# Routed rows scattered as sorted pieces of three rows, one indirect scatter a column

## What is computed

```python
logits = jnp.einsum('bsd,de->bse', x, gate_w) + gate_b
probs = jax.nn.softmax(logits, axis=-1)
top_probs, top_idx = jax.lax.top_k(probs, 2)          # 2 of 16 experts for each token
top_probs = top_probs / jnp.sum(top_probs, axis=-1, keepdims=True)
dispatch = jnp.sum(jax.nn.one_hot(top_idx, n_experts) * top_probs[..., None], axis=-2)
h1 = jnp.einsum('bsd,edh->bseh', x, w1)               # 64 -> 128
h2 = jnp.einsum('bsd,edh->bseh', x, w2)
hidden = jax.nn.silu(h1) * h2
expert_out = jnp.einsum('bseh,eho->bseo', hidden, w3) # 128 -> 64
out = jnp.einsum('bseo,bse->bso', expert_out, dispatch)
```

## Time and profile before

| | |
|---|---|
| median of 3 runs | 790.79 us (790.71 to 795.49) |
| profiled execution, span from first to last instruction | 791.9 us; no other time of this execution is given |
| mean granted TensorE clock, share of full speed | 0.873 |
| busy TensorE / its weight loads | 578.2 / 476.0 us |
| busy VectorE / ScalarE / GpSimd | 441.7 / 347.6 / 518.2 us |

### The profile page before, as it was taken

The page is one execution under the profiler, slowest core; times in us unless marked ns, Lnnn a source line. Parts: engine busy times, 40 slices in busy tenths (PEclk is TensorE's granted clock), DMA queues, the critical chain, the costliest instruction groups (busy, mean ns, idle before and its releaser), DMA issues.

```text
span 791.9 us, 14201 instructions
## 1 busy us (share of the span) xinstructions
PE 578.2 (73%) x3856; PEld 476.0 (60%) x3856; DVE 441.7 (56%) x1237; ACT 347.6 (44%) x753; POOL 518.2 (65%) x540
## 2 busy tenths in 40 slices
PE   5967796787799989998899889998958702883000
PEld 3455545574588678867786678687958702873000
DVE  5664755556447686676667567756765601454111
ACT  2124122152456476647564566446626701674111
POOL 2052246576771777777777777777777777777774
PEclk9976796798999999999999999979979965996555
DMA  2499022333553375528542744374345414544111
GB/s 78 101 229 396 28 71 83 97 97 90 148 170 89 72 188 142 144 53 208 136 124 69 190 130 121 76 175 109 112 117 128 114 51 127 135 100 98 40 40 31
DMA packets 168871, 93.20 MB, mean 118 GB/s; under 512 B 99680, under 2 KB 152928, under 8 KB 168800
## 3 DMA queue, kind: packets, MB, share of 16 engines
q1 hardware_dynamic: 151632, 66.71, 32.1%
q0 software_dynamic: 16384, 25.20, 11.6%
q10 hardware_dynamic: 784, 0.39, 0.2%
HBM read 45.06 MB, written 47.19 MB: 116 GB/s over the span
## 4 chain that ended last, share of the span: by engine, by line
POOL 33%; PE 29%; issue 15%; DVE 13%; DMA 7%; ACT 3%; POOLq 0%; ACTq 0%; DVEq 0%; SPq 0%
POOL rows_scratch L497 15%; POOL sums L514 14%; PE wide_ps L1030 5%; PE h_ps L1169 4%; PE y_ps L1186 3%; DMA hx<-xi_scratch 3%; DMA xi_scratch<-xi 2%; POOL hx L514 2%; POOL kexp L514 2%; PE turn_ps L1153 2%; PE wide_ps L1050 2%; PE wide_ps L1129 1%; PE hidT_ps L1179 1%; PE wide_ps L1036 1%; DVE twice_y L970 1%
## 5 line engine op out<-in xcount | busy, mean ns | idle before, releaser
L497 POOL DMA_INDIRECT rows_scratch<-z_parts,place x256 | 254.9, 996 | 128.4 <-issue 74.7
L514 POOL DMA_INDIRECT sums<-y_scratch,place x224 | 213.8, 955 | 82.7 <-issue 66.4
L1169 PE MATMUL h_ps<-w_hi,rowsT 128*128 x384 | 111.5, 320 | 40.9 <-DVE hid_all L972 33.8
L970 DVE SCALAR_TENSOR_TENSOR twice_y<-tanh,h_ps 128x256 f32<-128x256 f32 x192 | 79.8, 416 | 101.3 <-ACT tanh L618 85.3
L1169 PEld LDWEIGHTS h_ps<-w_hi,rowsT 128*128 128x128 f32 x384 | 74.6, 194 | 55.8 <-issue 54.5
L1186 PE MATMUL y_ps<-w_sb,hidT_all 128*128 x768 | 100.9, 276 | 1.1 <-ACT twice_y L631 1.1
L1169 PE MATMUL h_ps<-w_lo,rowsT 128*128 x384 | 101.0, 290 | 0.0
L1186 PEld LDWEIGHTS y_ps<-w_sb,hidT_all 128*128 128x128 f32 x768 | 97.4, 199 | 2.2 <-issue 2.2
L1153 PE MATMUL turn_ps<-ident,rows_all 128*128 128x128 f32 x384 | 60.8, 282 | 46.3 <-DMA rows_all<-rows_scratch 39.8
L618 ACT ACTIVATE tanh<-h_ps 128x256 f32<-128x256 f32 x192 | 69.8, 387 | 56.3 <-PE h_ps L1169 50.0
L972 DVE SCALAR_TENSOR_TENSOR hid_all<-twice_y,h_ps 128x256 f32<-128x256 f32 x192 | 80.8, 421 | 6.6
(11 more groups left out here) (252 smaller groups left out, 910.3 us busy)
## 6 DMA issues: line engine op xcount, KB each, us to landing
rows_all<-rows_scratch SPq DMA_DIRECT2D x96, 256.0 KB
y_scratch<-twice_y SPq DMA_DIRECT2D x96, 128.0 KB
rows_scratch<-tanh SPq DMA_DIRECT2D x3, 3072.0 KB, 19.4
xi_scratch<-xi SPq DMA_DIRECT2D x16, 256.0 KB
rows_scratch<-z_parts,place POOLq DMA_INDIRECT x256
hx<-xi_scratch SPq DMA_DIRECT2D x14, 256.0 KB
sums<-y_scratch,place POOLq DMA_INDIRECT x224
out<-sums SPq DMA_DIRECT2D x56, 64.0 KB
```

The costliest lines, as they stand in the source:

```text
L497: gp.indirect_dma_start(rows_dram[n], bass.IndirectOffsetOnAxis(ap=place[m % RING][:, r, j:j + 1], axis=0), z_parts[m % 2][:, j // 2, j % ...
L514: gp.indirect_dma_start(y_of[r][apart(m)][:, j // 2, j % 2, :], None, y_dram[m % 3], bass.IndirectOffsetOnAxis(ap=place[m % RING][:, r, j: ...
L970: ve.scalar_tensor_tensor(twice[:, j, :], tanh[:, j, :], 1.0, halves[:, j, 0, :], ALU.add, ALU.mult).then_inc(S["twice_done"], 1)
L1169: mm = te.matmul(h_ps[:, j * 256:(j + 1) * 256], rowsT[g % 2][:, j * P:(j + 1) * P], w[:, bass.ds(experts[g][j], 1), :, :].rearrange("d a ...
```

## The change

**Pieces.** A column's 256 routed rows (both copies of 128 tokens) are sorted by expert, and each expert's share is filled up to a multiple of three rows. That is at most (256 + 16 * 2) / 3 = 96 pieces of three rows. A piece is one element of the scatter: 3 x 512 bytes. A pair's tiles hold 42 pieces, 126 rows (R), and there are 13 groups of them a pair in place of 12, 104 in all. Pieces that hold nothing go to spare rows behind the tiles.

**Sorting.** `find_routes` on VectorE makes for each column a matrix of zeros and ones, 128 tokens x 288 sorted slots, in two operations (one for each copy). `move_rows` on TensorE multiplies the column's rows with it in three matmuls (one for each row of a piece, 96 x 128 out), into the bank that `hidT_ps` had. `take_piece` on ScalarE copies the 96 x 384 result to SBUF, and GpSimd scatters it in one indirect DMA in place of two. Four buffers of pieces and three of routes go round. Two columns a step (`ROUTES` counts half steps); pair 0 has four a step.

**Numbers of the places.** The 17 rank matmuls go; TensorE counts by column and expert, VectorE rounds the counts up to pieces, TensorE sums them (stage `base`), VectorE rounds up to tiles (`count_tiles`), TensorE adds the rest (stage `bases2`), and `find_ends` yields places, slots and piece numbers. There is one more turn between TensorE and VectorE. For pair 2 the stages from `rank` on come 3 steps later. The constants for this are made by some 25 GpSimd operations at the start (`sort_consts`), ahead of the split of the expert weights.

**Banks.** Turned rows and turned hidden rows now share `turn_ps`, so each turn waits for ScalarE's copy of the other, and project_out stands ahead of turn in the step.

**GpSimd's order.** The wait for TensorE's turn in each step is gone. A scatter waits for its own piece. The gathers of pair m are spread over 9 steps from step LAG + 13 m + 16, and those of the last pair stand in one step. The last expert group is in step 126 (before: 118).

Cut to its core:

```diff
+PIECE = 3
+PIECES = (2 * P + EXPERTS * (PIECE - 1)) // PIECE
+TILE_PIECES = P // PIECE
+R = TILE_PIECES * PIECE
 GROUP = 4
-GROUPS = 12
+GROUPS = 13
 TILES = GROUP * GROUPS
-assert TILES * P >= 2 * 2 * TOKENS + (EXPERTS - 1) * (P - 1)
-SLOTS = TILES * P
+assert PIECES <= P and TILES >= (COLS * PIECES + EXPERTS * (TILE_PIECES - 1)) // TILE_PIECES
...
              attend=10, added=10.5, squares2=10.5, ssq2=11, normed2=11.5, zturn=12.5, zparts=12.5, logits=13, pick=13.5,
-             rank=14, odds=15, count=14, base=14.5, ends=14.5, owner=15)
+             rank=17, odds=15, count=17, base=17.5, tiles=17.5, bases2=17.75, ends=18, owner=18.5)
...
-SPREAD = (6, 7, 7, 6)
-EVEN, GROUPS_NEXT = 4, 13
-SCATTER = (16, 22, 28, 44, 59, 72, 85, 98)
-GATHER = (38, 51, 65, 78, 91, 104, 111, 122)
-SUMS = [[43 + 14 * m + q for q in range(4)] for m in range(5)] + [[115, 116, 117, 118], [121, 121, 122, 122], [123, 124, 125, 126]]
+ROUTES = (29, 42, 64) + tuple(2 * (13 * m + 7) for m in range(3, PAIRS))
+GATHER = tuple(LAG + 13 * m + 16 for m in range(PAIRS))
+GATHER_STEPS = 9
+SUMS = [[GATHER[m] + (4 + 2 * q if m < PAIRS - 1 else 1 + q) for q in range(4)] for m in range(PAIRS)]
...
-ALONG = {4: ("att_ps_ready", 6), 8: ("k_ps_ready", 3), 12: ("logits_ps_ready", 2)}
...
-        hidT_ps = bank("hidT_ps")
+        piece_ps = bank("piece_ps")
         y_ps = bank("y_ps")
         wide_ps = bank("wide_ps", 1024)
         side_ps = bank("side_ps")
-        wides, sides = (wide_ps, h_ps), (side_ps, hidT_ps)
+        wides, sides = (wide_ps, h_ps), (side_ps, turn_ps)
...
+        def routes_at(half):
+            for m in range(PAIRS):
+                for j in range(COLS):
+                    if ROUTES[m] + (j // 2 if m == 0 else j) == half:
+                        yield m, j
...
-                wait_on(sp, scattered[m % 3], 16 * 2 * COLS * (m // 3 + 1))
+                if i == 0:
+                    wait_scattered(sp, m)
                 wait(sp, "rowsT_ps_ready", g - 2)
...
-                src = rows_dram[m % 3][i * GROUP * P:(i + 1) * GROUP * P, :].rearrange("(j s) (n e) -> s j n e", s=P, n=2)
-                sp.dma_start(rows[g % 3][:, :, :, :], src).then_inc(rows_in[g % 3], 16)
+                src = rows_dram[m % 3][i * GROUP * R:(i + 1) * GROUP * R, :].rearrange("(j s) (n e) -> s j n e", s=R, n=2)
+                sp.dma_start(rows[g % 3][0:R], src).then_inc(rows_in[g % 3], 16)
...
+            def sort_consts():
...
-                    wait(pool, "place_ready", m + 1)
-                    wait(pool, "z_split", m + 1)
+                    wait(pool, "piece_at_ready", m + 1)
                     if m >= 3:
                         wait(pool, "rowsT_ps_ready", GROUPS * (m - 2))
                     else:
                         pool.wait_ge(rows_zeroed[n], 16)
-                if m == 0 and j in ALONG:
-                    wait(pool, *ALONG[j])
-                for r in range(2):
-                    gp.indirect_dma_start(rows_dram[n], bass.IndirectOffsetOnAxis(ap=place[m % RING][:, r, j:j + 1], axis=0),
-                                          z_parts[m % 2][:, j // 2, j % 2, :, :].rearrange("p n e -> p (n e)").bitcast(F32),
-                                          None).then_inc(scattered[n], 16)
+                wait(pool, "piece_ready", COLS * m + j + 1)
+                gp.indirect_dma_start(pieces_dram[n], bass.IndirectOffsetOnAxis(ap=piece_at[m % 2][0:PIECES, j:j + 1], axis=0),
+                                      pieces[j % PIECE_RING][0:PIECES, :], None).then_inc(scattered[j % PIECE_RING], 16)
...
-                if 0 <= s - LAG < GROUPS_ALL:
-                    wait(pool, "rowsT_ps_ready", min(s - LAG + 2, GROUPS_ALL))
-                for m, j in scatters_at(s):
-                    scatter(m, j)
+                for half in (2 * s - 1, 2 * s):
+                    for m, j in routes_at(half):
+                        scatter(m, j)
...
+            def take_piece(m, j):
+                n = j % PIECE_RING
+                wait(act, "piece_ps_ready", COLS * m + j + 1)
+                wait_on(act, scattered[n], 16 * (COLS // PIECE_RING * m + j // PIECE_RING))
+                sc.activation(pieces[n][0:PIECES, :], piece_place(m, j)[0:PIECES, 0:PIECE * 2 * E], ACT.Copy).then_inc(S["piece_ready"], 1)
...
                     copy_hidT(g - 1)
+                for m, j in routes_at(2 * s - 1):
+                    take_piece(m, j)
                 for m, k in steps_at(s):
                     attend(m, k + 0.5)
                 for m in range(1, PAIRS):
                     if step_of(m, 0) - 1 == s:
                         turn_x(m)
+                for m, j in routes_at(2 * s):
+                    take_piece(m, j)
...
+            def find_routes(m, js):
+                for j in js:
+                    i = COLS * m + j
+                    wait(dve, "slot_ready", m + 1)
+                    wait(dve, "piece_ps_ready", i - ROUTE_RING + 1)
+                    ve.tensor_scalar(route[i % ROUTE_RING][:, :, :], slot_id[:, :, :], slot[:, 0, j:j + 1], None,
+                                     ALU.is_equal).then_inc(S["route_begun"], 1)
+                for j in js:
+                    i = COLS * m + j
+                    wait(dve, "route_begun", i + 1)
+                    ve.scalar_tensor_tensor(route[i % ROUTE_RING][:, :, :], slot_id[:, :, :], slot[:, 1, j:j + 1],
+                                            route[i % ROUTE_RING][:, :, :].bitcast(F32), ALU.is_equal, ALU.add).then_inc(S["route_ready"], 1)
...
+                for m, js in routes_of(2 * s):
+                    find_routes(m, js)
                 for m, k in steps_at(s):
                     attend(m, k + 0.5)
+                for m, js in routes_of(2 * s + 1):
+                    find_routes(m, js)
...
+                    wait(pe, "counted_spread", 2 * m + 2)
+                    wait(pe, "sort_consts_ready", 1)
+                    wait(pe, "same_expert_ready", 2)
+                    for n in range(2):
+                        te.matmul(side_ps[0:EXPERTS, 258:259], same_expert_b[:, :], counted_all[:, n, 0:1], start=(n == 0), stop=(n == 1))
+                    for n in range(2):
+                        te.matmul(side_ps[0:PIECES, 312:328], counted_all[:, n, 0:PIECES], to_first[:, n, :], start=(n == 0), stop=(n == 1))
+                    for n in range(2):
+                        te.matmul(slots, before_b[:, n, :], hot_b[:, :, :].rearrange("p j e -> p (j e)"), start=(n == 0), stop=False)
+                    for n in range(2):
+                        mm = te.matmul(slots, counted_all[:, n, :], to_slot[:, n, :, :].rearrange("p j e -> p (j e)"), start=False, stop=False)
+                    mm.then_inc(S["total_ps_ready"], 1)
+                    wait(pe, "piece_ready", COLS * m)
+                    for n in range(2):
+                        te.matmul(piece_ps[0:PIECES, :], counted_all[:, n, 0:PIECES], to_piece[:, n, :, :, :].rearrange("p a j e -> p (a j e)"),
+                                  start=(n == 0), stop=False)
+                if k == plan.bases2:
                     wait(pe, "tiles_spread", m + 1)
...
-                    wait(pe, "hot_sum_ready", m + 1)
-                    te.matmul(side_ps[0:EXPERTS, 256:257], hot_sum[:, :], ones[:, 0:1], start=True, stop=True)
-                    te.matmul(side_ps[:, 0:256], before_b[:, :], hot_b[:, :, :].rearrange("p j e -> p (j e)"), start=True, stop=False)
-                    for j in range(COLS - 1):
-                        mm = te.matmul(side_ps[:, (j + 1) * EXPERTS:256], ones_b[:, :],
-                                       hot_b[:, j, :].unsqueeze(1).broadcast_to([P, COLS - 1 - j, EXPERTS]), start=False, stop=False)
-                    mm.then_inc(S["rank_ps_ready"], 1)
+                    wait(pe, "hot_ready", 2 * m + 2)
+                    for n in range(2):
+                        mm = te.matmul(side_ps[:, 256 + n:257 + n], hot_b[:, n * BLOCKS:(n + 1) * BLOCKS, :].rearrange("p j e -> p (j e)"),
+                                       ones_b[:, 0:1], start=True, stop=True)
+                    mm.then_inc(S["counts_ps_ready"], 1)
...
+            def move_rows(m, j):
+                i = COLS * m + j
+                if j == 0:
+                    wait(pe, "z_split", m + 1)
+                    wait(pe, "piece_at_ready", m + 1)
+                    wait(pe, "mean_emb_ready", 1)
+                wait(pe, "route_ready", i + 1)
+                wait(pe, "piece_ready", i - 1 if m == 0 else i)
+                for n in range(PIECE):
+                    mm = te.matmul(piece_place(m, j)[0:PIECES, n * 2 * E:(n + 1) * 2 * E], route[i % ROUTE_RING][:, n, :],
+                                   z_parts[m % 2][:, j // 2, j % 2, :, :].rearrange("p n e -> p (n e)"), start=True, stop=True)
+                mm.then_inc(S["piece_ps_ready"], 1)
             def turn(g):
+                if g == 0:
+                    pe.wait_ge(S["owner_ready"], 2)
```

(14 more changed lines are left out.)

273 lines of the change are left out of this document (207 added, 66 removed).

## The result

| | before | changed |
|---|---|---|
| median of 4 runs each | 792.48 us (790.71 to 795.49) | 948.74 us (940.69 to 951.25) |
| profiled execution | 791.9 us | 945.4 us |
| mean granted TensorE clock | 0.873 | 0.827 |

The changed kernel is slower by a factor of 1.193 (95% interval 1.187 to 1.200). The forecast was 821 us, the range 784 to 866: the direction was right, the time is outside the range. Ratios are formed from runs in the fast state; the medians are of all runs, of which e7, e8, e16 and e20 have one each in the slow state, in e20 the profiled one.

A forecast was written before the change was run, and what follows sets the result against it. TensorE and GpSimd were taken to bound the kernel in turns. First group 167.1 + six groups 48 + five periods 420 + last stage 129 + tail 58.4 = 822.5, forecast as a median of 821 us, range 784 to 866.

The forecast's parts named there:

- What bounds the kernel before, and what GpSimd gives back: Whole kernel: TensorE and GpSimd bound it in turns; a relieved GpSimd can give back 73 us at most.
- The 16 us in the periods: Three middle 13-step periods, 352.2 to 589.9 us: GpSimd sets them, costing 16 us over a TensorE-bound 74 each.
- the 32 us wait for rows: Stage after attention work ends: TensorE sits 32 us until rows GpSimd scattered late are loaded; the change should remove it.
- the tail: From the last group's start to the end: 58.4 us in place of 77.2, with one pair's 32 gathers left.
- Prices of single operations: Added work: route operations 0.45 us each, a column's three move matmuls 0.375 us, ScalarE's piece copies 0.5 us.
- 74 + 6 for TensorE's matmuls + 4 for hand-overs with VectorE = 84: Each of five 13-step periods: TensorE-bound 74 us plus both additions, 420 us in all, range 77 to 91 each.
- Hidden: ScalarE's copies of pieces from PSUM: 8 us a period on an engine busy 45 of 75 us, adding nothing.
- 0, at most 0.3 us a step: Shared PSUM bank: in a 3.5 us step both copies end before the next turn, so almost no added wait.
- The last stage: 32 steps at 3.6 us, pair 7's columns 8 us, ScalarE 6 us: 129 us, range 118 to 140.
- the 6 us for ScalarE: Last stage: ScalarE weighs a pair's last quarter 36 us after its gathers begin, while 32 gathers take 40; 6 us added.
- For later pairs the two halves stand a step apart and are covered: Sort's second round trip between TensorE and VectorE: TensorE waits for pairs 0 and 1 only, not later ones.
- VectorE's chain rules the steps: Rival, shared with slow narrow float32r matmuls: a period of 90 us, about 858 us in all; chance 0.22 with the tail above.

The follow-up runs named there:

- e7: Changed kernel with one move matmul a column in place of three, for all pairs but the first: 938.14 us.
- e8: Changed kernel with expert numbers read early and, on VectorE, the new pair's keys' maximum ahead of the end of the choice before: 943.96 us.
- e16: Changed kernel without route operations, move matmuls and ScalarE's copies of pieces, for all pairs but the first: 857.34 us.
- e20: Kernel before with the move matmuls alone added, on constants: 799.64 us.
- e3: Kernel before with the shared bank alone, its waits, and the turn of rows behind project_out: 811.06 us.
- e22: Kernel before with shared bank, route operations, move matmuls and ScalarE's copies of pieces added, nobody reading the last three's results: 856.03 us.
- e23: Changed kernel without ScalarE's copies of the pieces, for all pairs but the first: 922.32 us.
- e1: Changed kernel with the next group's expert numbers read by TensorE's sequencer directly behind project_out, ahead of the turn of rows: 937.56 us.
- e19: Changed kernel with the hidden rows' turn of groups 78 to 103 in another bank, without the two waits: 938.69 us.
- e17: Changed kernel with two more matmuls, never read, at the start of each group but the first: 941.61 us.

## Why the prediction was wrong

- **What bounds the kernel before, and what GpSimd gives back**: right. 128 scatters at 0.977 us, the 32 us wait for rows gone, the tail 60.2 us (58.4). The 16 us in the periods can't be told apart in any run.
- **Prices of single operations**: right. Route operations 0.372 and 0.517 us (0.45 each), copies 0.485 (0.5); a column's move takes 0.31 us from its first matmul to the next instruction (0.375). In the kernel before, the moves made the two periods that TensorE sets 5.1 and 4.3 us longer (6.0), in an execution that took 6.8 us more than that run's median.
- **The step that failed: "74 + 6 for TensorE's matmuls + 4 for hand-overs with VectorE = 84"** (period 100.1, range 77 to 91). It prices two costs and puts the shared bank and the copies at nothing, and it takes all matmuls at the full clock. The runs in the kernel before showed in its place, over the mean of 77.1: the shared bank alone 80.7, routes, moves and shared bank 85.0, with the copies 89.9. The remaining 10 us, up to 100.1, stay open. Candidates are the longer choice and the dependence of route, matmul and copy on each other. e16 against e3 (85.6 and 80.7) points to about 5 us for the choice, with GpSimd's relief mixed in; no run took the choice by itself.
- **"Hidden" for ScalarE's copies**: wrong, for busy share was the wrong test. ScalarE is busy 50 of 100 us, and yet the copies cost 19 us (e22) to 28 us (e23). Each stands in line ahead of one that TensorE waits for, but TensorE's idle time grew little with them; its own matmuls took longer (e22).
- **"0, at most 0.3 us a step" for the shared bank**: wrong. I looked whether the copies end before the next turn; they do. I didn't ask what stands behind the waiting turn on TensorE's own sequencer. It costs 0.65 us a step without attention work, and +18.7 us alone in the kernel before.
- **The last stage, 156.2 us for 129**: the 12 steps that hold pair 7's columns took 69 us where the sum had 51, the 20 after them 87 where it had 72 (4.3 us a step in place of 3.6), and the 6 us for ScalarE did not show beside that. In this stage the cures gave back less than the step times promise: 8.1 us with e1, 5.1 with e19.
- **"For later pairs the two halves stand a step apart and are covered"** (the sort): wrong at one place, the end of the choice ahead of the keys' maximum. But moving it (e8) gained nothing.
- **No term for the clock.** Stage by stage it was 1.00 or near it where TensorE had little idle time, and I took matmul durations from there. With 7.5 us more idle time a period it fell to 0.80 to 0.90, and some 12 of the 23 us that a period grew are busy time beyond the added matmuls. What a full clock without filler would give back was not measured. The first group's 10 us are likely of this kind: the last 37 us of that stage had a clock of 0.63. This was not tried.
- **Rivals**: the chance for "VectorE's chain rules the steps" (858 us) was in the right direction, and too cheap as well. No run beat the kernel before; of the changed kernel's versions that compute all of it, e1 and e19 were the fastest, 11 and 10 us under it. That the change is slower was reasoned rightly; that the time is so far off was not one slip but several terms at nothing, all on the same side.

## What to carry to other kernels

When several engines hand each step's work to one another, ask of each added operation whether something that the critical engine waits for stands behind it in its queue. A busy share of 50% says nothing of that. Put the parts one by one into the old kernel before you trust a sum, and price each on the engines' queues, the sequencer's register reads among them. If TensorE gets new idle stretches, take its matmuls' durations from rows at its lower level too.

## What the runs showed of the hardware

- TensorE's clock: after a wait of 2.62 us the 16 matmuls from 554.79 us on took 3.44 us (1.91 before) and expert matmuls were 0.21 us apart instead of 0.12, with a granted clock of 0.50, which is the lower level of 1.2 GHz. 203 us of matmuls that nobody reads, put in the idle stretches and beyond, cost no time (e17). The Trainium skill ("TensorE: Matmul & The Clock Gate", section "HAM oscillation — how this bites in real kernels") tells of a matmul kernel whose waits for DMA let the clock fall again and again, so that each return is paid anew; the traces here agree in kind. The waits are others: for ScalarE and VectorE, and of 1 to 3 us, where the page's are for DMA and some 3 to 5 us long.
- Reading four register values for dynamic weights takes TensorE's sequencer 1.7 us from the load to the first matmul that uses them; eight queued matmuls cover all but 0.5 us of it, four leave 1.1 bare.
- A float32r matmul with 96 weight and 128 moving columns: three of them take 0.31 us at the full clock until the next instruction starts (592.55 to 592.86 in e8's profile), near 0.10 each, and 0.57 at the lower level (610.46 to 611.03 in the changed kernel's).
- A scatter of 96 rows of 1536 bytes takes GpSimd 0.977 us, one of 128 rows of 512 bytes 0.996: three times the bytes a row did not make its issue dearer.
